# Experts' MLPs: one gathered row per expert and partition, eight weight buffers, and a first layer whose result is turned by four transposes

## The reference, cut to what matters

```python
x = hidden_states.reshape(-1, c)                 # 4096 x 256
gates = softmax((x @ w_red) @ wg_n.T)            # 8 experts
scores, idx = max(gates), argmax(gates)
h = gelu(x @ W1[idx] + b1[idx])                  # W1: 8 x 256 x 512
o = (h @ W2[idx] + b2[idx]) * scores             # W2: 8 x 512 x 256
```

## Time and profile before

| | us |
|---|---|
| median of 3 runs | 3109.31 |
| the profiled execution | 3091.26 |
| its span | 3089.6 |
| PE, DVE, ACT, POOL busy in the span | 2725.4, 1650.3, 1176.2, 1675.6 |
| experts' MLPs, first to last instruction | 2131.0 to 2372.8 |
| first instruction of the stage behind it | 2376.15 |

### The profile page before, as it was taken

How to read it: one execution, slowest core, us unless ns; L and a number is a source line. 1 busy time by engine, 2 the same in 40 slices (tenths; PEclk the granted TensorE clock), 3 DMA queues, 4 the chain that set the end, 5 groups by cost and what they waited for, 6 DMA issues and landing times. The chain is left out here.

```text
span 3089.6 us, 41550 instructions
## 1 busy us (share of the span) xinstructions
PE 2725.4 (88%) x11761; PEld 1693.9 (55%) x11761; DVE 1650.3 (53%) x3283; ACT 1176.2 (38%) x1638; POOL 1675.6 (54%) x1418
## 2 busy tenths in 40 slices
PE   7999999999999999999999868862997488588696
PEld 5666666666666666666665433432996244334254
DVE  5565656566565656656566445660112555367853
ACT  3444444444444444444443325430111334244334
POOL 2666667676666666666676712217775412222343
PEclk9999999999999999999999889985998599799898
DMA  4323333323333332333333120024885200000143
GB/s 134 74 69 74 81 76 81 73 70 71 73 81 76 81 73 69 72 73 81 76 82 74 31 85 2 2 69 148 254 246 175 55 0 1 29 2 9 30 134 92
DMA packets 151413, 238.04 MB, mean 77 GB/s; under 512 B 30198, under 2 KB 75550, under 8 KB 151326
## 3 DMA queue, kind: packets, MB, share of 16 engines
q1 hardware_dynamic: 126510, 166.81, 21.8%
q0 software_dynamic: 20864, 64.06, 6.9%
q10 hardware_dynamic: 3952, 6.08, 0.6%
HBM read 89.52 MB, written 29.38 MB: 38 GB/s over the span
## 5 line engine op out<-in xcount | busy, mean ns | idle before, releaser
L636 POOL TENSOR_TENSOR a_total<-a_total,a_pr 128x1024 f32<-128x1024 f32 x384 | 911.8, 2374 | 70.0 <-ACT a_pr L620 49.6
L567 DVE TENSOR_REDUCE a_nmax<-a_psX 128x1 f32<-128x512 f32 x1024 | 693.7, 687 | 150.6 <-PE a_psX L562 147.9
L620 ACT ACTIVATE a_pr<-a_psS 128x1024 f32<-128x1024 f32 x512 | 524.7, 1026 | 653.3 <-PE a_psS L608 647.5
L648 PE MATMUL a_psO<-a_pr,a_vd 128*64 128x512 f32 x2048 | 481.8, 602 | 0.0
L636 POOL TENSOR_TENSOR a_total<-a_pr 128x1024 f32<-128x1024 f32 x64 | 152.8, 2388 | 511.3 <-ACT a_pr L620 511.3
L562 PE MATMUL a_psX<-a_kA,a_qA 128*128 128x512 f32 x1024 | 413.1, 404 | 8.5 <-DMA a_kA<-a_klo 5.1
L608 PE MATMUL a_psS<-a_qA,a_kA 128*128 128x512 f32 x1024 | 347.2, 420 | 1.6 <-DVE a_nT L583 1.4
L608 PE MATMUL a_psS<-a_qB,a_kB 128*128 128x512 f32 x1024 | 320.5, 394 | 1.4 <-DVE a_qB L591 1.4
L648 PEld LDWEIGHTS a_psO<-a_pr,a_vd 128*64 128x64 f32 x2048 | 129.9, 136 | 248.6 <-issue 212.1
L608 PEld LDWEIGHTS a_psS<-a_qA,a_kA 128*128 128x128 f32 x1024 | 184.5, 189 | 124.0 <-issue 90.1
L562 PEld LDWEIGHTS a_psX<-a_kA,a_qA 128*128 128x128 f32 x1024 | 192.1, 188 | 91.7 <-DVE a_nmax L567 16.4
(11 more groups left out here) (365 smaller groups left out, 4203.2 us busy)
## 6 DMA issues: line engine op xcount, KB each, us to landing
a_qA<-a_qhi SPq DMA_DIRECT2D x256, 128.0 KB, 2.3
a_kA<-a_khi SPq DMA_DIRECT2D x128, 128.0 KB, 2.3
a_kA<-a_klo SPq DMA_DIRECT2D x128, 128.0 KB, 2.3
a_kB<-a_khi SPq DMA_DIRECT2D x128, 128.0 KB, 2.3
a_qB<-a_qlo SPq DMA_DIRECT2D x128, 128.0 KB, 2.3
a_vd<-a_vg SPq DMA_DIRECT2D x128, 128.0 KB, 2.3
sorted_in<-g_zero SPq DMA_DIRECT2D x4, 1280.0 KB
e_xg<-sorted_in SPq DMA_DIRECT2D x40, 128.0 KB, 4.3
```

The lines of the kernel that those rows point to most:

```text
L567: w.eng.tensor_reduce(nmax[:, half, u:u + 1], psX[:, half, :], AX.X, ALU.max, negate=True)\
L620: w.eng.activation(pr[:, n, :], psS[:, half, :, :].rearrange("p a b -> p (a b)"), ACT.Exp, scale=SCALE)\
L636: w.eng.tensor_tensor(total[:, buf, :], first, pr[:, n, :], ALU.add).then_inc(sems["ad"], 1)
L648: last = w.eng.matmul(psO[q * HD:(q + 1) * HD, :], vd[:, b, kc, :], pr[:, n, q * 512:(q + 1) * 512], start=kc == 0, stop=kc == KC - 1)
```

## The change

Host side: W1, W2, b1 and b2 (b2 repeated for every partition) are laid side by side in one tensor `L0_ffn_W` with 8 x 128 rows of 2308 floats (9232 bytes). `fetch` then gathers one row per partition with one indirect DMA. There are 8 weight buffers in place of 4. `up` now has the tokens (xT) stationary and 512 columns of w1 moving, in two products (4 instructions); DVE copies the result (tokens x 512 hidden units) from psU to hh. A new step `turn_up` turns it by four PE transposes with a step of 4 elements into psH, and bias and GELU follow as before. The order in `tile(j)` becomes: `up` of tile j+2, `turn_up` of j+1, `turn` of j+3, `load` of j+4, `down` of j, `fetch` of j+8. NJ is rounded up to a multiple of 8, which is 40 again; the loop has 3 trips of 8 tiles.

```diff
-    SLOTS = 4
+    SLOTS = 8
+    LW = W.shape[1]
+    H = (LW - D) * P // (4 * P + 1)
+    HC = H // P
+    B1, B2 = 2 * H + HC * D, 2 * H + HC * D + HC
...
-        w1 = m.sb("w1", [P, SLOTS, 2, H])
-        w2 = m.sb("w2", [P, SLOTS, HC, D])
-        b1t = m.sb("b1t", [P, SLOTS, HC])
-        b2t = m.sb("b2t", [P, SLOTS, D])
+        wt = m.sb("wt", [P, SLOTS, LW])
+        hh = m.sb("hh", [P, 2, H])
+        psU = m.ps("psU", [P, 2, H])
...
-                for t, src, k in ((w1[:, slot, :, :].rearrange("p a h -> p (a h)"), w1r, 0),
-                                  (b1t[:, slot, :], b1r, 0),
-                                  (w2[:, slot, :, :].rearrange("p a c -> p (a c)"), w2r, 0),
-                                  (b2t[:, slot, :], b2, 1)):
-                    w.eng.indirect_dma_start(t, None, src, bass.IndirectOffsetOnAxis(ap=at[:, slot, k:k + 1], axis=0))\
-                        .then_inc(sems[f"w{slot}"], 16)
+                w.eng.indirect_dma_start(wt[:, slot, :], None, W, bass.IndirectOffsetOnAxis(ap=at[:, slot, 0:1], axis=0))\
+                    .then_inc(sems[f"w{slot}"], 16)
...
         def up
             if w.on("tensor"):
                 w.wait(f"w{slot}", w.at(f"w{slot}"))
                 w.wait("xt", w.at("xt", ahead))
+                w.wait("uc", w.at("uc", 1))
+                for c in range(2):
+                    last = w.eng.matmul(psU[:, par, :], xT[:, par, c, :], wt[:, slot, c * H:(c + 1) * H], start=c == 0, stop=c == 1)
+                last.then_inc(sems["u"], 1)
+            w.inc("u")
+            if w.on("vector"):
+                w.wait("u", w.at("u"))
+                w.wait("h", w.at("h", 1))
+                w.eng.tensor_copy(hh[:, par, :], psU[:, par, :]).then_inc(sems["uc"], 1)
+            w.inc("uc")
+
+        def turn_up(w, slot, later):
+            par = slot % 2
+            if w.on("tensor"):
+                w.wait("uc", w.at("uc", later))
                 w.wait("he", w.at("he", 1))
                 for a in range(HC):
-                    for c in range(2):
-                        last = w.eng.matmul(psH[:, par, a, :], w1[:, slot, c, a:H:HC], xT[:, par, c, :], start=c == 0, stop=c == 1)
+                    last = w.eng.transpose(psH[:, par, a, :], hh[:, par, a:H:HC], ident[:, :])
                 last.then_inc(sems["h"], 1)
...
         def tile(w, j, slot, left=SLOTS):
             par = slot % 2
+            if left >= 2:
+                up(w, (slot + 2) % SLOTS)
             if left >= 1:
-                up(w, (slot + 1) % SLOTS)
-            if left >= 2:
-                turn(w, par)
+                turn_up(w, (slot + 1) % SLOTS, 1 if left >= 2 else 0)
             if left >= 3:
-                load(w, j + 3, 1 - par)
+                turn(w, 1 - par)
+            if left >= 4:
+                load(w, j + 4, par)
             down(w, j, slot, 1 if left else 0)
             if left >= SLOTS:
                 fetch(w, j + SLOTS, slot)
...
             load(w, 2, 0)
             turn(w, 1)
+            load(w, 3, 1)
             up(w, 0, 1)
+            up(w, 1)
+            turn(w, 0)
+            turn_up(w, 0, 1)
```

More of the change, by code:

```diff
@@ L2382, in _, with expert_mlps @@
             walk(Writer(nc, eng, "tensor", sems))
-def expert_mlps(nc, xs, rows, W1, b1, W2, b2, os):
-    E, _, H = W1.shape
+def expert_mlps(nc, xs, rows, W, os):
     NJ = rows.shape[1]
+    SLOTS = 8
+    LW = W.shape[1]
+    H = (LW - D) * P // (4 * P + 1)
     HC = H // P
-    SLOTS = 4
-    w1r = W1.rearrange("e (p a) h -> (e p) (a h)", a=2)
-    w2r = W2.rearrange("e (p a) c -> (e p) (a c)", a=HC)
-    b1r = b1.rearrange("e (p a) -> (e p) a", a=HC)
+    B1, B2 = 2 * H + HC * D, 2 * H + HC * D + HC
     with ExitStack() as ctx:
@@ L2398, in expert_mlps @@
         ident = m.sb("ident", [P, P])
-        w1 = m.sb("w1", [P, SLOTS, 2, H])
-        w2 = m.sb("w2", [P, SLOTS, HC, D])
-        b1t = m.sb("b1t", [P, SLOTS, HC])
-        b2t = m.sb("b2t", [P, SLOTS, D])
-        at = m.sb("at", [P, SLOTS, 2], I32)
+        wt = m.sb("wt", [P, SLOTS, LW])
+        at = m.sb("at", [P, SLOTS, 1], I32)
         xg = m.sb("xg", [P, 2, D])
         xT = m.sb("xT", [P, 2, 2, P])
+        hh = m.sb("hh", [P, 2, H])
         hT = m.sb("hT", [P, 2, HC, P])
@@ L2410, in expert_mlps @@
         psT = m.ps("psT", [P, 2, 512])
+        psU = m.ps("psU", [P, 2, H])
         psH = m.ps("psH", [P, 2, HC, P])
         psO = m.ps("psO", [P, 2, 512])
-        sems = {n: m.sem(n) for n in ("cst", "w", "x0", "x1", "w0", "w1", "w2", "w3", "cp", "id", "tr", "xt", "h", "he", "o", "od", "st0", "st1")}
+        names = ["cst", "w", "x0", "x1", "cp", "id", "tr", "xt", "u", "uc", "h", "he", "o", "od", "st0", "st1"]
+        sems = {n: m.sem(n) for n in names + [f"w{k}" for k in range(SLOTS)]}
         block = ctx.enter_context(nc.Block())
@@ L2427, in fetch @@
                 w.wait("od", w.at("od"))
-                w.eng.tensor_copy(at[:, slot, :], rows[:, bass.ds(j, 1), :].rearrange("p a b -> p (a b)")).then_inc(sems["cp"], 1)
+                w.eng.tensor_copy(at[:, slot, :], rows[:, bass.ds(j, 1), 0]).then_inc(sems["cp"], 1)
                 w.wait("cp", w.at("cp", -1))
@@ L2431, in fetch @@
                 w.eng.tensor_tensor(idle[:, :], one[:, :], one[:, :], ALU.add).then_inc(sems["id"], 1)
-                for t, src, k in ((w1[:, slot, :, :].rearrange("p a h -> p (a h)"), w1r, 0),
-                                  (b1t[:, slot, :], b1r, 0),
-                                  (w2[:, slot, :, :].rearrange("p a c -> p (a c)"), w2r, 0),
-                                  (b2t[:, slot, :], b2, 1)):
-                    w.eng.indirect_dma_start(t, None, src, bass.IndirectOffsetOnAxis(ap=at[:, slot, k:k + 1], axis=0))\
-                        .then_inc(sems[f"w{slot}"], 16)
+                w.eng.indirect_dma_start(wt[:, slot, :], None, W, bass.IndirectOffsetOnAxis(ap=at[:, slot, 0:1], axis=0))\
+                    .then_inc(sems[f"w{slot}"], 16)
             w.inc("cp")
             w.inc("id")
-            w.inc(f"w{slot}", 64)
+            w.inc(f"w{slot}", 16)
         def turn(w, par):
@@ L2451, in turn @@
                 w.wait("tr", w.at("tr"))
-                w.wait("h", w.at("h", 1))
+                w.wait("u", w.at("u", 1))
                 w.eng.tensor_copy(xT[:, par, :, :].rearrange("p a t -> p (a t)"), psT[:, par, 0:2 * P]).then_inc(sems["xt"], 1)
@@ L2472, in up @@
                 for a in range(HC):
-                    last = w.eng.activation(hT[:, par, a, :], psH[:, par, a, :], GELU, bias=b1t[:, slot, a:a + 1])
+                    last = w.eng.activation(hT[:, par, a, :], psH[:, par, a, :], GELU, bias=wt[:, slot, B1 + a:B1 + a + 1])
                 last.then_inc(sems["he"], 1)
@@ L2482, in down @@
                 for a in range(HC):
-                    last = w.eng.matmul(psO[:, par, 0:D], hT[:, par, a, :], w2[:, slot, a, :], start=a == 0, stop=a == HC - 1)
+                    last = w.eng.matmul(psO[:, par, 0:D], hT[:, par, a, :], wt[:, slot, 2 * H + a * D:2 * H + (a + 1) * D], start=a == 0, stop=a == HC - 1)
                 last.then_inc(sems["o"], 1)
@@ L2489, in down @@
                 w.wait(f"w{slot}", w.at(f"w{slot}"))
-                w.eng.tensor_tensor(ob[:, par, :], psO[:, par, 0:D], b2t[:, slot, :], ALU.add).then_inc(sems["od"], 1)
+                w.eng.tensor_tensor(ob[:, par, :], psO[:, par, 0:D], wt[:, slot, B2:B2 + D], ALU.add).then_inc(sems["od"], 1)
             w.inc("od")
@@ L2706, in two_layers @@
     NT = TOK // P
-    E = a["L0_ffn_W1"].shape[0]
+    E = a["L0_ffn_W"].shape[0] // P
     y = nc.dram_tensor("y_scratch", (TOK, D), F32, kind="Internal").ap()
-    NJ = (NT + E - 1 + 3) // 4 * 4
+    NJ = (NT + E - 1 + 7) // 8 * 8
     sorted_in, sorted_out = (nc.dram_tensor(n, (NJ * P, D), F32, kind="Internal").ap() for n in ("sorted_in", "sorted_out"))
@@ L2720, in two_layers @@
             sort_by_expert(nc, X, xT, a["L0_ffn_w_red"], a["L0_ffn_wg"], score, pos, rows, sorted_in)
-        expert_mlps(nc, sorted_in, rows, *[a["L0_ffn_" + n] for n in ("W1", "b1", "W2", "b2")], sorted_out)
+        expert_mlps(nc, sorted_in, rows, a["L0_ffn_W"], sorted_out)
         with ExitStack() as ctx:
@@ L2759 @@
         data[n + "Wo"] = wo.reshape(2, 2, 4, 16, d).transpose(0, 2, 1, 3, 4).reshape(d, d)
-    for n in ("w_red", "wg", "W1", "b1", "W2", "b2"):
+    for n in ("w_red", "wg"):
         data["L0_ffn_" + n] = i["L0_ffn_" + n]
+    w1, b1, w2, b2 = (i["L0_ffn_" + n] for n in ("W1", "b1", "W2", "b2"))
+    E = w1.shape[0]
+    wide = [w1.reshape(E, 128, -1), w2.reshape(E, 128, -1), b1.reshape(E, 128, -1), np.broadcast_to(b2[:, None, :], (E, 128, d))]
+    data["L0_ffn_W"] = np.concatenate(wide, axis=2).reshape(E * 128, -1)
     for n in ("W_qkv", "b_qkv", "W_out", "b_out"):
```

## The result

| | before | after |
|---|---|---|
| median of 10 runs each, interleaved | 3100.84 (3094.63 to 3110.63) | 3083.30 (3077.66 to 3096.73) |
| the profiled execution | 3091.26 | 3086.83 |
| its span | 3089.6 | 3085.1 |
| experts' stage, its first instruction to the first of the next stage | 245.1 | 230.8 |
| the rest of the span | 2844.5 | 2854.3 |

The ratio is 0.9946, interval 0.9929 to 0.9962: 17.5 us of median, faster. 3080 was predicted, from a gain of 29 us on a median of 3109.3; on the median of these ten runs the same gain would have read 3072. The sign and the bound were right, and 12 us of the gain are missing. That 3080 lies only 3 us from the measured 3083 is in part luck: the three runs that I started from were 8.5 us above the median of ten, and this covers most of the missing gain.

A forecast was written before the change was run, and what follows sets the result against it. PE was taken to bound the kernel at 5.58 us a tile, then the token load; 2146 + 188 (38 tiles of 4.95) + 4.4, with 5 us more for the fill, gave 29 us gain: 3109.3 - 29 = 3080, range 3057 to 3104.

The forecast's parts named there:

- The bound behind PE: Experts' stage: with PE faster, the token load is late next, PE waiting 0.2 to 0.7 us for it each tile.
- Up: PE's up-products per tile: 4 instructions of 430 ns, 1.72 us instead of 3.63.
- turn_up: PE's four added transposes with a step of 4: 0.9 us per tile taken, 0.44 the lower bound.
- The token loop's length: Turn, issue and landing of the one token load in flight: 5.0 us at the median landing; tile period taken as 4.95.
- The rival with a period of 5.7: Token loop lands at 5.7 us a tile, gain mostly lost: gain 5 us, 3104; chance 0.10.
- The fill: Stage start: tile 2's weights come at 2146.5; token loads pass a full q0, about 4 tiles at 6.2, 5 us more.
- The DMA engines as a bound: DMA engines moving 1.45 MB per tile in the experts' stage need 4.7 to 4.9 us a tile.
- One gather: POOL's weight fetch: one gather instead of four, 1.7 us per tile instead of 5.4; without it PE's gain stops at 5.4.
- Four steps that cost nothing: Per tile: DVE's copy 0.68 us hidden, POOL 1.7, ScalarE unchanged at 1.1, waits on `u` and `uc` covered by 2.8.
- The rival of large packets: Token loads wait behind 9232-byte weight packets: loop 6.2 to 6.6 us, 14 us slower, 3123; chance 0.08.
- The clock: Rival: a third of the tiles at PE's 1.2 GHz level, 39 us lost, about 3119; chance 0.03.
- a sign of being wrong: One of the listed signs against the forecast: a granted PE clock under 0.95 in the experts' stretch.

The follow-up runs named there:

- e1: The changed kernel with four token buffers in place of two, tokens loaded three tiles earlier: 3039.49, ratio 0.9787 against the kernel before.
- e3: The kernel before with only the merged row (one gather), keeping four weight buffers, the old order and the old up: 3087.63, ratio 0.9946 against before.
- e4: The changed kernel with before's four gathers per tile, keeping eight buffers and the new products: 3086.95, ratio 0.9949 against the kernel before.
- f4: The changed kernel with the weight row cut into three gathers of 4096, 4096 and 1040 bytes: 3093.87, ratio 0.9891 against the kernel before.
- g2: The changed kernel run again unchanged, on another chip: 3086.13, ratio 0.9863 against the kernel before in the same batch, stage 240.3 us.
- f3: The changed kernel with four token buffers and four weight buffers in place of eight: 3147.88, ratio 1.0056 against the kernel before.

## Why the prediction was right or wrong, point by point

- **The bound behind PE: right.** The token load was named as what is late next, with waits in each tile on `e_xg<-sorted_in`. There are 26, and e1, which changes only the token loads, removes them. They are 1.4 us each, where 0.2 to 0.7 was expected.
- **Up: right.** 1.72 predicted, 1.72 measured (2181.78 to 2183.50). The reading of the earlier trace rows, loading paced the old up, fits.
- **turn_up: mis-sized, on the bound that I didn't take.** I took 0.90 because today's weight loads with the step of 4 cost 227 ns; it takes 0.46, the price of the turn's transposes, though each of the four loads a stationary operand with that step. So the step alone doesn't cost 227 ns; that this is the price of loading for a float32 product is my guess, which no run separates. It had little effect on after, whose PE floor of 4.15 mostly hides under the token loop; e1 gains some 16 us more by it than with the floor of 4.57 (38 x 0.42).
- **The token loop's length: the term that was mis-sized.** Predicted 4.95 a tile, and 193 us for the 38 tiles with the fill's charge. Measured some 208, 5.5 each (from 2150.79 to PE's end near 2363, less the end's 4.4). These 15 us are what is missing of the forecast 29, and leave the 14 between the two profiles. The 30 tiles from 2173.96 to 2340.83 take 5.56, where the sum had 0.62 + 4.3. The largest part is the landing. The view's 4.3 is not that of the 40 loads: it times 20 of them, those of one of the two buffers. By the semaphore records of all 40 the median is 4.6 us, before and after alike, and the mean over these 30 tiles is 4.64, 0.34 more than I used. From the turn to the issue it is 0.70 on the mean instead of 0.62, and from landing to turn 0.04. The clock, below, adds 0.12. Only 0.05 comes from tiles in which the landing is early and PE binds; they are three of the thirty, at 4.3 us. The rival with a period of 5.7 (3104, no measurable gain) named this loop and had a chance of 0.10. The measured period, 5.5, lies at the upper edge of the forecast's own 4.7 to 5.5.
- **The fill: right in its start, low in its charge.** up(2) starts 14.4 us after the stage's start, 15.0 predicted. But eight queued gathers delay a token load to 8.4 us, where I had bounded by before's 5.5: two tiles of 8.9 and 7.8 us. The four tiles from 2153.05 take 26.7 us, where the charge had 4 x 6.2 = 24.8. What I took as the DMA engines' best, 295 GB/s, was what POOL's issues asked of them; they do 404 to 416.
- **The DMA engines as a bound (4.7 to 4.9): wrong, without effect.** e1 does a tile in 4.15. Share of busy time at low load was no capacity: in after, q0's 57.4% of 16 engines over the 226 us makes 405 ns for each packet of 9232 bytes, where 215 ns for 4096 would make 485. The Trainium skill, DMA: Bandwidth & Descriptors (section Bandwidth), puts the ceiling of the 16 ports at 435 GB/s; the fill's 416 lies just under it.
- **One gather: "worth the fill's 1 to 2 us, and the release of POOL" was wrong.** It alone brought 18 us (e3). I read PE's waits in the earlier trace rows as all that the tokens cost, and left out the 18 tiles over 5.58; e3 has an undisturbed tile nearly every time. That before's profiled execution is 9.6 us under its median does not excuse this: its stage of 245.1 is not known to be short, and the part outside, 2844.5, is the shortest of all profiles. What the prediction had right is that without it the new products' gain stops near 5.4 (e4).
- **Four steps that cost nothing, as predicted:** DVE's copy, 692 ns against 683, behind PE; POOL, 1.7 us of 5.5; ScalarE, 46 us of the stage; the waits on `u` and `uc`, which appear in no row of waits.
- **The rival of large packets: false.** A row is one packet as it feared, but the median landing didn't rise (4.6 before and after), e3's loads land at 3.8, and f4's small packets bring at most some tenths of a us per tile. The rule that a DMA engine changes queues only at a packet's end may hold; no run here shows its effect.
- **The clock: given 0.03 as a rival, and put at nothing in the sum; it costs some 4 us.** The mean of 0.97 hides four stretches of 3.4 us at the 1.2 GHz level. They came behind waits for a token: 4.5 us (to 2161.90), 2.1 (to 2214.65), 1.9 (to 2232.07) and 2.1 (to 2313.69), though the wait of 2.1 to 2169.70 had none behind it. The second of them, in the timeline and in the stretch (columns as in the earlier trace rows):
```profile
2214.65 0.51 PE L2442 MATMUL e_psT<-e_ident,e_xg 128*128 128x128 f32 x2 [2.14 <-DMA e_xg<-sorted_in]
2214.99 2.71 PE L2493 MATMUL e_psO<-e_wt,e_hT 128*128 128x256 f32 x8
2217.49 2.80 PE L2459 MATMUL e_psU<-e_wt,e_xT 128*128 128x512 f32 x4
```
```profile
2215.93:2219.34 3.41, 3.41 (x8) 2.02 (x7) 0.42 (x1) 0.00 (x0) 0.36 (x2) 0.50 0.46 185
```
Down and up take 5.1 us there instead of 3.45. In the last three of the four the next token had landed 0.8 to 1.8 us before its turn, so it was the clock that made the tile 5.95 long. g2 has seven such stretches and a granted clock of 0.94 over its tiles, under the 0.95 that I had named as a sign of being wrong, and some 4 of the 9.5 us by which its stage is longer are from there. e1, which has no such waits, is at 1.00 with six transposes in each 4.15 us. The statement of the Trainium skill, TensorE: Matmul & The Clock Gate (part 4, PE-mode transpose), that they don't count as work, is neither borne out nor refuted by this. In f3, where waits reach 4 us and come in every other tile, the clock costs more (0.85).

## What to carry to other kernels

When the bounding engine gets faster, look at every load that waits for a step of the loop and is waited for one tile later: at 5.58 us a tile it cost a few us, at 4.15 it took two thirds of the gain, and keeping four loads in flight instead of one gave 44 us. See first whether a load can be issued earlier into a buffer that is already free. Before a median landing goes into a sum, ask how many of the transfers it times. Compare tile periods too, not only the waits, for the waits view showed 1.9 us where the tiles had lost 6. And a change of two parts is to be tried with each part alone, and on more than one chip: here each alone gave the whole on one, and not on another.

## What the runs showed of the hardware that wasn't expected

- An indirect gather's rows of 9232 bytes become one packet each, and a fourth of the instructions moves the same 1.18 MB: a gather takes 0.98 us of POOL with rows of 9232 bytes, and 0.95 with a bias of 16.
- One core kept 331 GB/s over 151 us and 404 to 416 in the fill.
- Four float32 transposes that read with a step of 4 take 0.46 us; eight float32 products with 128 moving columns and the same step in the stationary operand take 3.63.
- Waits of some 2 us, one in a tile, can be followed by 3.4 us at half the clock, which a mean of 0.97 over 203 us does not show.
- The same kernel before takes 22 us more on two chips than on a third, nearly all within a stage of many small gathers (26 us between its two profiles), while e1 differs by 0.7 us. Why semaphores arrive late there is open. Not tried: two token buffers with two loads in flight, three token buffers, and four gathers spaced out over the tile.
